# Feed-forward: the transfers of the accumulator and of the output issued from ScalarE instead of SyncE

## What is computed

```python
x = _layernorm(x + _L0_attn_ref(x), axis=-1)
x = _layernorm(x + _L0_xattn_ref(ctx_4096, ctx_4096, x), axis=-1)
x = _layernorm(x + _L0_ffn_ref(x, W_base, gate_W, A, B), axis=-1)
```

## Time and profile before

| | |
|---|---|
| time, median of 3 runs | 2012.11 us (2011.35 to 2013.47) |
| the profiled execution's own time | 2017.59 us |
| its span, first to last instruction | 2015.8 us |
| granted TensorE clock, mean | 0.966 |
| PE busy | 1803.6 us, 89% of the span |
| VectorE busy | 1460.8 us, 72% |
| ScalarE busy | 798.1 us, 40% |
| GpSimd busy | 295.8 us, 15% |
| DMA queue q1 (all that SyncE issues) | 86.1% of 16 engines' time, 455.15 MB |

### The profile page before, as it was taken

The page is one execution under the profiler, slowest core; times in us unless marked ns, Lnnn a source line. Parts: engine busy times, 40 slices in busy tenths (PEclk is TensorE's granted clock), DMA queues, the critical chain, the costliest instruction groups (busy, mean ns, idle before and its releaser), DMA issues. The chain is left out here.

```text
span 2015.8 us, 27865 instructions
## 1 busy us (share of the span) xinstructions
PE 1803.6 (89%) x10466; PEld 968.4 (48%) x10466; DVE 1460.8 (72%) x2679; ACT 798.1 (40%) x970; POOL 295.8 (15%) x450
## 2 busy tenths in 40 slices
PE   3898989999963969999999999997599999999997
PEld 2666666666630434445444554443244444444443
DVE  4777787878759867767667767797667767776773
ACT  5777777676635222222222212242322232223221
POOL 3344444535310000000000000000000010001000
PEclk9999999999985989999999999998799999999999
DMA  8899998898749399889998978647999999999993
GB/s 272 214 294 264 294 264 258 230 269 231 211 168 232 100 225 236 198 210 230 239 215 196 221 183 213 159 146 214 220 255 253 262 239 261 255 262 238 266 255 117
DMA packets 648371, 457.06 MB, mean 227 GB/s; under 512 B 590816, under 2 KB 594912, under 8 KB 627424
## 3 DMA queue, kind: packets, MB, share of 16 engines
q1 hardware_dynamic: 648224, 455.15, 86.1%
HBM read 221.78 MB, written 85.98 MB: 153 GB/s over the span
## 5 line engine op out<-in xcount | busy, mean ns | idle before, releaser
L1541 PE MATMUL bank_f<-w_hi_f,a_cols_f 128*128 128x512 f16 x3584 | 1097.5, 383 | 108.6 <-DMA a_cols_f<-rows_f 66.5
L1541 PE MATMUL bank_f<-w_lo_f,a_cols_f 128*128 128x512 f16 x1792 | 686.3, 383 | 0.0
L1541 PEld LDWEIGHTS bank_f<-w_hi_f,a_cols_f 128*128 128x128 f16 x3584 | 353.2, 99 | 545.8 <-issue 53.5
L1541 PEld LDWEIGHTS bank_f<-w_lo_f,a_cols_f 128*128 128x128 f16 x1792 | 176.5, 99 | 204.4 <-issue 6.4
L1134 ACT ACTIVATE rows_f<-xn_f 128x1024 f16<-128x1024 f32 x93 | 98.3, 1057 | 385.1 <-DMA xn_f<-x_scratch 155.2
L1134 ACT ACTIVATE rows_f<-sums_f 128x1024 f16<-128x1024 f32 x93 | 98.0, 1054 | 333.7 <-DMA a_cols_f<-rows_f 326.4
L1309 DVE SCALAR_TENSOR_TENSOR y_f<-bank_f,w_iscale,y_f 128x512 f32<-128x512 f32 x192 | 135.0, 745 | 122.9 <-PE bank_f L1541 89.3
L1270 DVE TENSOR_TENSOR rows_f<-sums_f,rows_f 128x1024 f16<-128x1024 f32 x93 | 113.6, 1221 | 104.9 <-ACT rows_f L1134 104.9
L666 PE MATMUL ps_s_fast<-k_both_fast,q_hi_fast 128*128 128x256 f16 x1024 | 170.0, 274 | 6.2 <-DMA k_both_fast<-v_lo_fast 5.2
L1309 DVE SCALAR_TENSOR_TENSOR y_f<-bank_f,w_iscale_f,y_f 128x512 f32<-128x512 f32 x192 | 134.5, 742 | 42.9 <-PE bank_f L1541 42.8
L524 DVE SCALAR_TENSOR_TENSOR x2buf_fast<-ps_c_fast,iscale_fast,xbuf_fast 128x512 f32<-128x512 f32 x128 | 96.0, 750 | 70.6 <-PE ps_c_fast L655 70.0
(11 more groups left out here) (212 smaller groups left out, 2538.9 us busy)
## 6 DMA issues: line engine op xcount, KB each, us to landing
xbuf_fast<-x SPq DMA_DIRECT2D x32, 1024.0 KB, 6.2
x_scratch<-x2buf_fast SPq DMA_DIRECT2D x32, 1024.0 KB, 6.4
y_f<-x_scratch SPq DMA_DIRECT2D x32, 1024.0 KB, 6.8
xn_f<-x_scratch SPq DMA_DIRECT2D x62, 512.0 KB, 4.7
xn<-x_scratch SPq DMA_DIRECT2D x60, 512.0 KB, 6.0
cbuf<-ctx_in SPq DMA_DIRECT2D x16, 1024.0 KB, 5.8
cbuf_fast<-ctx_in SPq DMA_DIRECT2D x16, 1024.0 KB, 7.0
cbuf<-w_chunks SPq DMA_DIRECT2D x16, 1024.0 KB, 5.5
```

Source lines behind the costliest of these rows:

```text
L1541: ins = nc.tensor.matmul(bank[i][:], a_cols[:, i, part + kk, :], ww[:, W_SLOT[i], kk, :], start=(kk == 0 and part == 0 and ww is w_hi), st ...
```

## The change

The functions `load_residual`, `store_first`, `load_first`, `rows_out` and `store_out` move from SyncE's block to ScalarE's, with the same waits and the same semaphores, and the calls move with them. ScalarE calls `store_first(s - 1)` and, in slot 16, `load_first` after `high_rows` 1; `store_out(s - 1)` directly after `normalise(s - 1)`; `load_first` after `high_rows` 2; `load_residual(s + 1)` after `high_rows` 3. The turns, the loads of x2 and of weights, and the transfers of h stay with SyncE.

```diff
@@ SyncE @@
-                def load_residual(s):
...
-                def store_first(s):
...
-                def load_first(s):
...
-                def store_out(s):
...
                 turn(0, 6)
                 load_b(0)
-                load_residual(0)
                 load_unit(6)
...
                 for s in range(SLOTS):
-                    if 1 <= s <= NP_:
-                        store_first(s - 1)
                     if s == LAST:
                         for u in range(HK, HK + 3):
                             load_unit(u)
                         store_h(s)
-                        load_residual(s + 1)
...
                             load_block(s + 1, b)
-                        load_first(s)
                     turn(s + 1, 0)
                     turn(s + 1, 1)
-                    if s > NP_:
-                        store_out(s - 1)
                     turn(s + 1, 2)
-                    if s > NP_:
-                        load_first(s)
                     turn(s + 1, 3)
                     next_block(s + 2, A21)
-                    load_residual(s + 1)
                     turn(s + 1, 4)
...
-                store_out(SLOTS - 1)
-                for i in range(2):
-                    sp.wait_ge(y_stored[i], 16 * (SLOTS // 2))
-                sp.wait_ge(first_stored, 16 * NP_)
@@ ScalarE @@
+                def load_residual(s):
+                    if s < SLOTS:
+                        if s == 0:
+                            act.wait_ge(w_lo_done, 3 * 4)
+                        elif s == 1:
+                            act.wait_ge(w_lo_done, 3 * HK)
+                        else:
+                            act.wait_ge(y_stored[s % 2], 16 * (s // 2))
+                        if s:
+                            act.wait_ge(added, NU * (s - 1) + 1)
+                        c = s // NP_
+                        act.dma_start(y[s % 2][:], x2[...]).then_inc(residual, 16)
+                def store_first(s):
+                    act.wait_ge(added, NU * (s + 1))
+                    act.dma_start(y_scratch[token(s)], y[s % 2][:]).then_inc(y_stored[s % 2], 16)
+                def load_first(s):
+                    if s == NP_:
+                        act.wait_ge(w_lo_done, 3 * 2 * HK)
+                        for i in range(2):
+                            act.wait_ge(y_stored[i], 16 * (NP_ // 2))
+                    else:
+                        act.wait_ge(first_stored, 16 * (s - NP_))
+                    act.dma_start(y_first, y_scratch[token(s)]).then_inc(first_loaded, 16)
+                def store_out(s):
+                    act.wait_ge(normalised, 2 * (s - NP_) + 1)
+                    act.dma_start(rows_out(s, 0), y_first).then_inc(first_stored, 16)
+                    act.wait_ge(normalised, 2 * (s - NP_) + 2)
+                    act.dma_start(rows_out(s, 1), y[s % 2][:]).then_inc(y_stored[s % 2], 16)
...
                 b_high(0)
+                load_residual(0)
                 router_exp(0)
...
                     if s == LAST:
+                        store_first(s - 1)
                         router_exp(s)
...
                         copy_h(s)
+                        load_residual(s + 1)
                         for u in range(HK + 2, 2 * HK):
                             unit_high(u)
                         continue
...
                     high_rows(s + 1, 1)
+                    if 1 <= s <= NP_:
+                        store_first(s - 1)
+                    if s == NP_:
+                        load_first(s)
                     if s > NP_:
                         normalise(s - 1)
+                        store_out(s - 1)
                     if 1 < s < LAST:
                         router_exp(s)
                     high_rows(s + 1, 2)
+                    if s > NP_:
+                        load_first(s)
                     high_rows(s + 1, 3)
+                    load_residual(s + 1)
                     if 1 < s < LAST:
                         copy_h(s)
...
                 normalise(SLOTS - 1)
+                store_out(SLOTS - 1)
+                for i in range(2):
+                    act.wait_ge(y_stored[i], 16 * (SLOTS // 2))
+                act.wait_ge(first_stored, 16 * NP_)
```

More of the change, by code:

```diff
@@ L977, in load_b @@
                         sp.dma_start(b_raw[ps][i * ER:(i + 1) * ER, :], b_rows[:, ps * HL:(ps + 1) * HL]).then_inc(b_loaded, 16)
-                def load_residual(s):
[L981 to L992, removed]
-                def store_first(s):
-                    sp.wait_ge(added, NU * (s + 1))
-                    sp.dma_start(y_scratch[token(s)], y[s % 2][:]).then_inc(y_stored[s % 2], 16)
                 def store_h(s):
@@ L1002, in store_h @@
                     sp.dma_start(h_scratch[token(s)], flat[:, 256:512].bitcast(BF16)).then_inc(h_moved, 16)
-                def load_first(s):
-                    if s == NP_:
-                        sp.wait_ge(w_lo_done, 3 * 2 * HK)
-                        for i in range(2):
[L1009 to L1012, removed]
                 def load_h(s):
@@ L1019, in load_h @@
                         sp.dma_start(flat[:, 256:512].bitcast(BF16), h_scratch[token(s)]).then_inc(h_moved, 16)
-                def rows_out(s, c):
-                    return out[bass.ds(2 * token(s) * P, 2 * P), c * HL:(c + 1) * HL].rearrange("(t p) c -> p t c", p=P)
-                def store_out(s):
[L1026 to L1029, removed]
                 wait_stored(sp, x2_stored, NP_)
@@ L1180, in copy_h, with rows_out @@
                     nc.scalar.activation(h_t, ps_h, ACT.Copy).then_inc(ht_copied, 1)
+                def load_residual(s):
[9 more added lines that the diff above has]
+                        c = s // NP_
+                        act.dma_start(y[s % 2][:], x2[bass.ds(2 * token(s) * P, 2 * P), c * HL:(c + 1) * HL].rearrange("(t p) c -> p t c", p=P)
+                                     ).then_inc(residual, 16)
+                def store_first(s):
[9 more added lines that the diff above has]
+                    act.dma_start(y_first, y_scratch[token(s)]).then_inc(first_loaded, 16)
+                def rows_out(s, c):
+                    return out[bass.ds(2 * token(s) * P, 2 * P), c * HL:(c + 1) * HL].rearrange("(t p) c -> p t c", p=P)
+                def store_out(s):
[3 more added lines that the diff above has]
+                    act.dma_start(rows_out(s, 1), y[s % 2][:]).then_inc(y_stored[s % 2], 16)
                 def normalise(s):
```

## The result

The changed kernel takes 2116.48 us (2098.72 to 2128.99), the kernel before 2012.79 us on the same chip: ratio 1.0492, 95% interval 1.0453 to 1.0531. I had forecast 1998 us, with 1986 to 2034 us as the range. It is slower by 104 us, and by a mechanism that none of my cases worked out.

A forecast was written before the change was run, and what follows sets the result against it. PE was taken to bound the first half, nearly full DMA the second. Terms 0 + 0 - 3 - 2.5 - 10 + 1 = -14.5 us from the 2012.1 us median gave 1997.6, say 1998 us; range 1986 to 2034 us.

The forecast's parts named there:

- the cover named: First half, slots 0 to 15: PE busy 400 of 400 us, so moving the store and residual load costs 0.
- the first term, 0: Slots 15 to 17: turn 0 earlier, but `load_first` waits for a store on ScalarE; 0, bounds -3 to +3 us.
- The pause of 4.82 us before 1403: Start of second half: residual load goes out earlier on ScalarE's queue, so the turn ending PE's pause lands sooner; -3 us.
- ScalarE's own costs: Plain second-half slots: about 0.5 us later at `high_rows` 2, up to 1.2 us at `high_rows` 3, residual's wait covered.
- The end: Last two stores: on ScalarE the first is issued only after the last ACTIVATE is dispatched; +1 us.
- the plain slots: Second half, 12.7 slots up to 1950 us: no copy-turn handover in one queue; 0.8 us gained a slot, -10 us.
- the pause of 21.18 us: PE's pause until 1449.91: turns no longer wait for all of an earlier copy; -2.5 us, bounds 0 to 7 us gained.
- C: Slower: copy issues on ScalarE held 2.5 us each while a turn is pushed; +22 us, 2034 us, chance 0.30.
- Its last sentence but one: In C: a slowdown would also follow if turns came off worse than copies in the sharing; no size given.
- B: Nothing moves: same bytes, full engines, turns' gain lost by copies or given back by ScalarE's waits; 2012 us, chance 0.20.
- A: The forecast: two queues overlap, so turns are issued and land sooner in the second half; 1998 us, chance 0.50.
- A's lower end: A with the pause of 21.18 us shortened by the full 7 us and all slots at 38.2 us: 1987 us.

The follow-up runs named there:

- waits_only: Kernel before with all DMAs still on SyncE; ScalarE waits as in the changed kernel, except ahead of `store_first` in the first half: ratio 0.9986.
- stores_only: Kernel before with only `store_first` and `store_out` moved to ScalarE's queue, both loads staying on SyncE: ratio 0.9997.
- first_load_only: Kernel before with only `load_first`, the load of y_first, moved to ScalarE's queue: 2046.7 us, ratio 1.0121.
- gate2: Changed kernel, but in the second half SyncE issues turn 2 only when y_first has landed: ratio 1.0128 to the kernel before.
- first_load_4k: As `first_load_only`, but y_first is loaded in two DMAs with rows of 4 KB instead of one with 8 KB: ratio 1.0117 to the kernel before.

## Why the prediction was wrong

**What held.** The first half cost nothing, under the cover named, PE busy all the time. In slots 15 to 17 the first term, 0, holds: the store that ScalarE waits for costs it hardly more than turn 0 did (5.41 us of waiting ahead of the next item, 4.91 before). The pause of 4.82 us before 1403 shrank: the gap between the starts of two matmuls there is 2.3 us in the changed kernel against 5.2, so -2.9 for my -3. ScalarE's own costs were right: 0.52 us ahead of `high_rows` 2 (forecast about 0.5) and waits for the first store of 9.1 us in 500 in the changed kernel, below the 1.2 us a slot allowed. `waits_only` confirms the sum of them as 0.

**The end** was forecast at +1 us and is 0. The first of the last two stores was issued 1.01 us before the last ACTIVATE started, in both kernels (2103.32 and 2104.33 after, before): on ScalarE's list too the DMA, which comes behind that ACTIVATE, was issued before it had started.

**The step that failed** is in the plain slots: "The gain can be nothing (full engines) or 1.2 us a slot". Its lower bound was zero, and with the same assumption in the pause of 21.18 us ("the sum of the work is the same"). I took two queues to share the engines without loss, and the only question to be how the gain is divided. The 94.4 us of the spans split into 13.3 us by the start of slot 18 (1463.22 against 1449.91) and 81.1 us after it, 5.8 us for each of 14 slots, where I had written -0.8. With the pause it was the same: +14.2 us, not -2.5. I had put that pause down to turn 4; in the changed kernel ScalarE's longest wait in it, 21.48 us until 1449.16, is for turn 2.

What was missing is a look at *what is under way at the moment of the new issue*. My text has the times: y_first "is loaded from 1748 instead of 1751.60", and turn 2 was issued at 1746.34, the store of y at 1744.13 with 6.6 us to land. I read that as an earlier, so harmless, load. No row of the kernel before has a turn beside a copy on another queue, since it has one queue, so a loss should have been bounded from rows too, and the bound could only be wide. After the fact: a turn lands in 4.6 us alone and in 6.9 behind copies, so +2.3 us for each of the turns that meet a copy, three a slot, +7 us. That would have taken in 5.8.

**The rivals.** C had the right sign and the wrong mechanism. Its price was a hold of 2.5 us at each issue on ScalarE; the issues took 0.34 to 0.45 us in the whole kernel, also the 58 of 96 that went out while SyncE was pushing a turn. Its last sentence but one, that turns could come off worse than copies in the sharing, was the place for the true case, and it had neither a price nor a place. B, no change, is what the stores, the residual alone and the waits did. It is what the Trainium skill says on the DMA: Bandwidth & Descriptors page under "Issuing engines are not separate DMA queues", that transfers from several engines interleave on the same DMA engines and only issue time is saved. `stores_only` agrees with 0.9997, and `first_load_only` does not, at 1.0121, with the same bytes: there the measurement decides.

**The signs I had named** were in part right as tests. "The forecast is wrong as a whole if turns beside copies land later than 6.9 us": turn 2 landed in 16.8, and PE's count fell to 1861. But three signs of A came in although A was wrong: the pause before 1403 is 1.9 us (below 2), and over all turns of 1450 to 1950 us the median issue took 3.2 us (below 4.98) and the median landing 5.8 us (below 6.9), since a few late turns do not move a median.

**What stays open.** Why the engines crawl at 48 to 175 GB/s after store, turn and load have been issued so, while their share is 0.99 to 1.41 (in the changed kernel; 0.60 over the 4 us of 89 GB/s); the runs show the condition, not the reason. Why the residual behind the load delays turn 2 by 2.6 us more (17.5 against 14.9), which beyond the slack makes 50 us in all. And whether the turn must be the second of the three: no run had another order with all three overlapping, since in `gate2` the turn went out only when the load had landed.

Two sums of the prediction are slightly off, without weight for the forecast: A's lower end comes to 1988 us by its own terms (-3, -7, -15 and +1), not 1987, and the residual's earlier issue to 7 us (1758.28 - 1751.2), not 6.

## What to carry to other kernels

A second DMA queue does not only change who waits for whom, it changes which transfers are in the engines at the same time, and in this case two queues moved less than one at the same busy share; so read GB/s beside the share, and landing times of single transfers beside their medians. When a DMA moves to another queue, write down what is under way at its new moment of issue, and give that overlap a loss bound as well as a gain. Find the slack of each transfer that others wait for: here turn 2 could land 4 us late for nothing, and the rest was paid in full. If it turns out badly, move the issue by a few microseconds before giving the queue up: here that was the difference between +4.9% and -0.4%.

## What the runs showed of the hardware that was not expected

- A DMA transpose was pushed behind a store of 1 MB, and a load of 1 MB issued from another queue with that store some 3 us from landing. Once the store had landed, the engines moved 89 GB/s over 4 us (`first_load_only`) and 48 GB/s over 6 us (changed kernel, with the residual's load too), against 386 to 398 GB/s while the store drained and 206 GB/s for a turn alone; the transpose landed in up to 22.2 us in the slot shown. Any two of the three without the third did not do this in the runs.
- In `first_load_only` the load's first packet came a median 4.7 us after its issue, and 4.8 us when GpSimd issued it; in the kernel before it was 1.2 us, and in `gate2`, with the same store under way but no turn behind it, 1.9 us.
- Stores on the second queue cost nothing beside transposes, although the first of them goes out 1.0 us (median) after a transpose: ratio 0.9997.
- A DMA issue took 0.34 to 0.45 us of ScalarE's list in the changed kernel, and no issue there was held by SyncE's push of a transpose (the time that its issue instruction takes), though one went out during a push of 13.1 us. The longest on ScalarE in any run was 1.5 us, in `first_load_4k`.
